# Attention: probabilities turned by VectorE, value products on 32x64 tiles, rope by swap and GpSimd

## The reference

```python
x: (4, 1024, 256), 16 heads, nope 128, rope 64, values 128, rank 64
q = x @ Wqa @ Wqb ; ckv = x @ Wkva
compressed, k_pe = ckv[..., :64], ckv[..., 64:]
kv = compressed @ Wkvb            # k_nope, v for each head
q_pe, k_pe = _rope(q_pe), _rope(k_pe)
scores = einsum('bhnd,bhmd->bhnm', qf, kf) / sqrt(192)
attn = softmax(where(causal, scores, min))
out = einsum('bhnm,bhmd->bhnd', attn, v) ; x = x + out @ Wout
x = x + ffn(layernorm(x))         # 8 groups x 8 experts, top 8
```

## Time and profile before

| | us |
|---|---|
| median of 3 runs | 1732.25 (1731.49 to 1733.08) |
| the profiled execution | 1732.48 |
| its span, first to last instruction | 1730.7 |
| preparation and start, to the first body | 90 |
| first body | 27.2 |
| thirty bodies, 117.2 to 1183.6 us | 1066.4 |
| last scores and router, to 1240 us | 56.4 |
| experts, to the end | 491 |

### The profile page before, as it was taken

The page is one execution under the profiler, slowest core; times in us unless marked ns, Lnnn a source line. Parts: engine busy times, 40 slices in busy tenths (PEclk is TensorE's granted clock), DMA queues, the critical chain, the costliest instruction groups (busy, mean ns, idle before and its releaser), DMA issues.

```text
span 1730.7 us, 31809 instructions
## 1 busy us (share of the span) xinstructions
PE 1662.5 (96%) x11024; PEld 1357.5 (78%) x11024; DVE 1248.5 (72%) x2923; ACT 955.1 (55%) x2255; POOL 509.9 (29%) x433
## 2 busy tenths in 40 slices
PE   5799999999999999999999999999999999999998
PEld 4667777777777777777777777777699999999998
DVE  6888888888888788888888888888654554555543
ACT  6566666666666666666666666666433333433332
POOL 4543334323333333423343333335310110110100
PEclk9899999999999999999999999999999999999999
DMA  8300010012000003000002210001300000000000
GB/s 287 117 26 20 20 32 25 20 47 96 20 25 20 20 32 111 26 20 26 25 26 65 65 32 24 22 19 38 110 1 25 26 1 25 26 14 12 13 13 13
DMA packets 50204, 68.49 MB, mean 40 GB/s; under 512 B 8512, under 2 KB 33088, under 8 KB 50048
## 3 DMA queue, kind: packets, MB, share of 16 engines
q1 hardware_dynamic: 50048, 66.45, 11.6%
HBM read 52.00 MB, written 14.42 MB: 38 GB/s over the span
## 4 chain that ended last, share of the span: by engine, by line
PE 81%; issue 8%; DVE 4%; ACT 2%; DMA 1%; POOL 1%; ACTq 0%; DVEq 0%
PE aps L43 46%; PE fps L43 23%; PE aps L1233 9%; PE fps L1618 2%; ACT probs L1307 1%; DVE f_stats L739 1%; DMA raw_down<-in_down 1%; DVE nmax L1357 0%; POOL rot L1454 0%; PE fps L700 0%; PE fps L668 0%; DVE aTl L1759 0%; DVE rot L1371 0%; DVE aps L1357 0%; DVE rot L792 0%
## 5 line engine op out<-in xcount | busy, mean ns | idle before, releaser
L1307 ACT ACTIVATE probs<-aps,nmax 128x384 f32<-128x384 f32 (+7 forms) x512 | 378.6, 743 | 229.7 <-DVE nmax L1357 224.0
L1357 DVE CUSTOM_DVE_ANT_0 aps<-aps,mask_row 128x384 f32<-128x384 f32 (+7 forms) x512 | 387.2, 772 | 105.9 <-PE aps L43 100.3
L1233 PE MATMUL aps<-ident,probs 128*128 128x128 f32 x2304 | 324.0, 272 | 0.9 <-ACT probs L1307 0.6
L43 PE MATMUL aps<-kTh,qh 128*128 128x512 f32 (+3 forms) x768 | 293.3, 382 | 23.3 <-ACT probs L1307 18.4
L1233 PEld LDWEIGHTS aps<-ident,probs 128*128 128x128 f32 x2304 | 271.7, 140 | 27.2 <-issue 1.5
L1318 ACT COPY pT<-aps 128x512 f32<-128x512 f32 (+3 forms) x485 | 229.5, 504 | 92.1 <-PE aps L1233 89.5
L43 PE MATMUL aps<-pT,v 128*64 128x512 f32 (+3 forms) x1536 | 268.9, 492 | 0.6 <-ACT pT L1318 0.6
L43 PE MATMUL aps<-kTl,qh 128*128 128x512 f32 (+3 forms) x768 | 257.9, 343 | 0.0
L1454 POOL TENSOR_TENSOR rot<-rot 64x512 f32<-64x512 f32 x128 | 163.9, 1280 | 211.8 <-DVE rot L1371 211.8
L43 PE MATMUL aps<-kTh,ql 128*128 128x512 f32 (+3 forms) x768 | 221.8, 343 | 0.0
L43 PEld LDWEIGHTS aps<-pT,v 128*64 128x64 f32 x1536 | 101.7, 136 | 152.1 <-issue 142.1
(11 more groups left out here) (190 smaller groups left out, 2878.1 us busy)
## 6 DMA issues: line engine op xcount, KB each, us to landing
linv_b<-inverses_scratch SPq DMA_DIRECT2D x128, 128.0 KB, 2.8
wqs<-wq_scratch SPq DMA_DIRECT2D x30, 256.0 KB, 3.1
raw_numbers<-in_x SPq DMA_DIRECT2D x8, 512.0 KB, 6.2
acc<-in_x SPq DMA_DIRECT2D x8, 512.0 KB, 4.0
inverses_scratch<-linv_t SPq DMA_DIRECT2D x256, 1.0 KB
x_scratch<-acc SPq DMA_DIRECT2D x8, 512.0 KB, 2.9
x<-x_scratch SPq DMA_DIRECT2D x8, 512.0 KB, 3.9
out<-x SPq DMA_DIRECT2D x7, 512.0 KB, 2.9
```

Of the source, the lines that this page charges most:

```text
L43: return nc.tensor.matmul(out, lhsT, rhs, start=start, stop=stop, skip_group_check=True)
L1233: last = nc.tensor.transpose(tps[:, TS.index(x) % 3, j * P:(j + 1) * P], probs[c][:, c * (pair % 2), a, off:off + P], t.ident[:])
L1307: nc.scalar.activation(probs[c][:, c * (r % 2), a, off:off + w], sps[:, at:at + w], ACT.Exp, bias=nmax[:, c, a, j:j + 1], scale=-1.0, accu ...
L1357: nc.vector.tensor_tensor_reduce(out=s, in0=s, in1=mask[:, N - PW[c][j]:N], scale=-1.0, scalar=3.0e38, op0=ALU.add, op1=ALU.min, accum_out ...
```

## The change

- **Turning.** T and OUT are gone. TURN(c, a, j) on VectorE is one instruction for each score tile: it transposes `probs` in blocks of 32 x 32 from SBUF to SBUF, into `pT_first` or `pT_second`. A 32-row strip of `pT` then holds, for 32 of each 128 tokens, the keys in blocks of 32. `probs` becomes a ring of five tiles.
- **Value products.** The values are held four times, one copy for each 32-row strip (`vrep`), loaded from DRAM in pieces of 256 bytes. A product has 32 rows (keys) and 64 columns (values), and 32 to 128 moving columns; strip a writes bank 4 + a, head h the upper or lower 64 partitions: eight tiles of the array. There are 360 such products in a body (two PE instructions each) where there were 24, and they stand in PV(1, 0 to 7) and PV(0, 0 to 3), twelve pieces of four key blocks. O reads the four banks.
- **Rope.** RAW on ScalarE copies the projection to `rot1`; SWAP, two transfers of 64 KB on SP, crosses the halves into `rot2`; ROT is three instructions of 64 partitions on GpSimd (on VectorE for the first two queries).
- **Transfers.** Keys, values and `acc` move in 256 KB pieces, one or two a body, at set places of SP's list. `acc` is double. All four batches' values go to DRAM.
- **The first expert weights** are split by ScalarE and VectorE in the last body instead of GpSimd.
- All tables are written anew. Scores keep to banks 0 to 3 but for the last tile and the first body.

The core of the diff:

```diff
+    nc.vector.transpose(pT[c][:, a, 0:w // S32, j * S32:(j + 1) * S32],
+                        probs[:, SLOT[EXP(c, a, j), r], 0:w].rearrange("p (b k) -> p b k", k=S32))\
+        .then_inc(p_turned, 1)
...
-                    for kb in range(first, first + n):
-                        for a in range(2):
-                            k = TS.index(T(c, kb, a))
-                            s = t_cols(TS[k])
-                            last = mm(nc, ops[64 * a:64 * a + 64, s:QC], t.v32[:, pair // PAIRS % 2, kb, :],
-                                      pT[:, k % PT_BUFS, s:QC], kb == 0, kb == KB[c] - 1)
+                    if part == 0:
+                        if pair % PAIRS == 0:
+                            pe.wait_ge(values_loaded[b % 2], 64 * (b // 2 + 1))
+                        pe.wait_ge(p_turned, last_of("tr", c, pair))
+                        banks_free(x)
+                    n = BLOCKS[c] // PARTS[c]
+                    for b in range(part * n, (part + 1) * n):
+                        for a in range(4):
+                            s = max(0, b // 4 - 4 * c) * S32
+                            if b // 4 >= 4 * c and b % 4 > a:
+                                s += S32
+                            if s == 4 * S32:
+                                continue
+                            for h in range(2):
+                                last = mm(nc, banks[64 * h:64 * h + 64, OB + a, s:4 * S32],
+                                          vrep[32 * a:32 * a + 32, pair // PAIRS % 2, b, :],
+                                          pT[c][32 * a:32 * a + 32, h, b, s:], b == 0, b == BLOCKS[c] - 1)
...
-                    nc.vector.tensor_tensor(rot1[:, k, :], sps[:, at:at + QC], t.cosT[:, cols], ALU.mult)
-                    for to, source in ((0, 32), (32, 0)):
-                        last = nc.vector.tensor_tensor(rot2[to:to + 32, k, :], sps[source:source + 32, at:at + QC],
-                                                       t.sinT[to:to + 32, cols], ALU.mult)
+                    nc.scalar.copy(rot1[:, rot_slot(x, r), :], banks[:, bank_of(Q(c, a), r), :]).then_inc(q_raw, 1)
...
+            def swap(x, r):
+                sp.wait_ge(q_raw, count(of("raw", x), r))
+                sp.dma_start(rot2[0:32, k, :], rot1[32:64, k, :]).then_inc(q_swapped[k], 16)
+                sp.dma_start(rot2[32:64, k, :], rot1[0:32, k, :]).then_inc(q_swapped[k], 16)
...
+            eng.wait_ge(q_swapped[k], 32 * ((count(of("raw", x), r) + 1) // 2))
+            eng.tensor_tensor(rot2[:, k, :], rot2[:, k, :], t.sinT[:, cols], ALU.mult).then_inc(q_turned, 1)
+            eng.tensor_tensor(rot1[0:64, k, :], rot1[0:64, k, :], t.cosT[0:64, cols], ALU.mult).then_inc(q_turned, 1)
+            eng.wait_ge(q_turned, 2 * n)
+            eng.tensor_tensor(rot1[0:64, k, :], rot1[0:64, k, :], rot2[:, k, :], ALU.add).then_inc(q_add, 1)
...
+            def load_values(b, a):
+                sp.dma_start(vrep[32 * a:32 * a + 32, b % 2], t.v_dram[b].rearrange("(n k) d -> k n d", k=S32))\
+                    .then_inc(values_loaded[b % 2], 16)
...
+        POOL = [ROT(1, 1), ROT(1, 0), LOW(1, 1), LOW(1, 0), ROT(0, 0), ROT(0, 1), OLOW(1), LOW(0, 1), LOW(0, 0),
+                OLOW(0)]
+        SYNC = [SWAP(1, 1), SWAP(1, 0), KEEP(1), SPREAD(1), SWAP(0, 0), KEEP(0), SPREAD(0), SWAP(0, 1)]
```

More of the change, by code:

```diff
@@ L1014, in exists, with body @@
             return 0 <= r + age(x) < B * PAIRS
-        BODIES = range(-1, B * PAIRS + 1)
-        def body(order, first, r):
+        BODIES = range(-1, LAST + 1)
+        def body(order, first, last, r):
+            if r == LAST:
+                return last
             return [x for x in (first if r == 0 else order) if exists(x, r)]
         def tensor_body(r):
-            return body(TENSOR, TENSOR_FIRST, r)
-        TS = [x for x in TENSOR if x[0] == "t"]
-        PVS = [x for x in TENSOR if x[0] == "p"]
@@ new lines, in sync_body @@
+        def sync_body(r):
+            return body(SYNC, SYNC_FIRST, SYNC_LAST, r)
+        SS = [x for x in TENSOR if x[0] == "s"]
+        COUNT, KINDS = {}, {}
+        for bodies in (tensor_body, vector_body, scalar_body, pool_body, sync_body):
+            for r in BODIES:
+                for x in bodies(r):
+                    if x[0] not in ("router", "mask", "stats", "quad"):
+                        KINDS[x[0]] = KINDS.get(x[0], 0) + 1
+                        COUNT[x, r] = KINDS[x[0]]
@@ new lines, in count, with of, at_pair, last_of @@
+        def count(x, r):
+            return COUNT[x, r]
+        def of(kind, x):
+            return (kind,) + x[1:]
+        def at_pair(x, pair):
+            return count(x, pair - age(x))
+        def last_of(kind, c, pair):
+            return max(at_pair(x, pair) for x in TENSOR + VECTOR + SCALAR if x[0] == kind and x[1] == c)
+        RING_USERS = [(x, r) for r in BODIES for x in scalar_body(r) if x[0] == "exp"]
+        SLOT = {y: n % RING for n, y in enumerate(RING_USERS)}
+        def slot_before(x, r):
+            n = RING_USERS.index((x, r))
+            return RING_USERS[n - RING] if n >= RING else None
@@ L1069, in bank_users, with takes_banks @@
+        def takes_banks(x):
+            return x[0] in ("s", "q", "y", "router", "mask") or x[0] == "p" and x[2] == 0
+        USERS = {bank: [(x, r) for r in BODIES for x in tensor_body(r) if takes_banks(x) and bank in banks_of(x, r)]
+                 for bank in range(8)}
         def bank_users(x, r):
@@ new lines, in load_acc, with store_acc, all_added @@
+            def load_acc(b, n):
+                tiles = slice(2 * n, 2 * n + 2)
+                sp.dma_start(acc[:, 1 - b % 2, tiles, :], x_v[b][:, tiles, :]).then_inc(acc_loaded[b % 2], 16)
+            def store_acc(b, n):
+                tiles = slice(2 * n, 2 * n + 2)
+                sp.dma_start(x2_v[b][:, tiles, :], acc[:, 1 - b % 2, tiles, :]).then_inc(x2_stored, 16)
+            def all_added(pair):
+                for c in range(NC2):
+                    sp.wait_ge(y_added, last_of("acc", c, pair))
@@ L1129, in _ @@
+            job = {"spw": keep_inverses, "spr": spread_inverses, "sw": swap}
+            sp.dma_start(mask[:, N - P:N], ins["mask"]).then_inc(mask_loaded, 16)
+            for r in BODIES:
+                if r == 0:
+                    sp.wait_ge(t.values_stored, 32)
+                    for a in range(4):
+                        load_values(0, a)
+                if 1 <= r and r + 1 < LAST:
+                    queries_of_second_half(r - 1)
                     if r <= 2:
@@ L1176, in _ @@
+            scores_of(LAST - 1)
+            queries_of_second_half(LAST - 1)
+            load_experts(nc, t, ins, 1, slice(0, 4))
+            all_added(LAST - 1)
+            for n in range(4):
+                store_acc(B - 1, n)
         @block.tensor
@@ L1477, in run @@
                         router_norm(nc, t, 1, i)
-                for x in body(POOL, POOL_FIRST, r):
+                job = {"rot": rot_job, "low": low_job, "olow": olow_job, "stats": stats_job}
+                for x in pool_body(r):
                     job[x[0]](x)
-                    if r == LAST - 1 and x == LOW(1, 0):
-                        pool.wait_ge(q_ps, max(count(Q(1, a), LAST - PAIRS - 1) for a in range(2)))
+                    if r == LAST - 1 and x == [y for y in pool_body(r) if y[0:2] == ("low", 1)][-1]:
+                        pool.wait_ge(q_ps, max(at_pair(Q(1, a), LAST - PAIRS - 1) for a in range(2)))
                         router_root(nc, t, 0)
```

599 lines of the change are left out of this document (288 added, 311 removed).

## The result

The changed kernel takes 1660.5 us (median of 4 runs, 1657.6 to 1665.4) against 1732.3 us: ratio 0.959 (0.957 to 0.961). The forecast was 1588 us. So it is faster, inside the range and on the side that was given 0.78, but only half as much as forecast: 72 us instead of 144. The profiled execution took 1660.9 us. One of the four executions of the variant fetch_b (2047.8 us, granted clock 0.65) was in a slower state of the chip and is left out.

The account below looks back on a forecast made before the run. TensorE sets the body period, 35.5 us falling to 30.9 (30.35 + 0.2 + 0.35); over 31 bodies 143 us, last body -4, start +3: 1732.5 - 144 = 1588 us. Range 1540 to 1750, the forecast's own bounds 1540 to 1640.

Parts of the forecast that it names:

- rival A: TensorE in each piece: tiles do not overlap enough; with four at once the kernel takes about 1787 us; chance 0.08.
- rival B: VectorE's turns cost two cycles a column, 37.4 us a body and the bound, kernel 1790 us; chance 0.06.
- D: Full queues: VectorE at 92% in strict order, waits for it leave bodies of 33 to 35 us, 1655 to 1715; chance 0.08.
- The low end for the tiles: TensorE's 720 value-product instructions cost 7.7 us a body, all eight tiles at once, against 28.2 with only two.
- together 11.5 us: New value products on TensorE per body: 7.7 us columns, 0.4 for 32-column blocks, 3.4 for nine visits.
- nine visits: TensorE's separate entries into the narrow shape in a body: 0.38 us each, 3.4 us.
- the diagonal blocks: Eight 32-column blocks on TensorE, whose 27 ns may be shorter than the load of 64 weights: 0.4 us.
- the prediction's own signs of being wrong: PE waiting on turns or low parts in every body, or narrow visits costing more than 0.4 us each.
- rows 5: Cited TensorE trace rows: four tiles at once, four products lasting 0.43 us together, weight loads some 7 ns a pair.
- 0.8 + 0.2 + 0.35: Idle in the forecast period, us: PE's old idle 0.8, query chain 0.2, costlier hand-overs with VectorE at 92% 0.35.
- rival C: Rope chain before the second-half scores becomes the path, 12.6 us against 12.7 of cover: 1620 to 1680 us; chance 0.20.
- 4.6 us to 31 bodies: Period falling from 35.5 to 30.9 us, counted for 31 bodies: 143 us in sum.

Follow-up runs that it names:

- fetch_b: Changed kernel, implied TensorE waits dropped, body padded to 6.5 blocks of 256 instructions, 100 more instructions ahead of the first scores: 1646.0 us (ratio 0.951).
- narrow: Changed kernel with all value products but those of block 0 cut to their last 32 columns: 1666.8 us, one execution.
- slow_low: even_c with the low part of the second half's first query computed twice on GpSimd: 1682.1 us (ratio 0.971).
- joined: Changed kernel with the pieces of value products in six visits instead of nine: 1708.8 us (ratio 0.987).
- even_c: Changed kernel with fulfilled waits padding a body to exactly 7 blocks (1792 instructions), 68 more instructions ahead of the first scores: 1644.8 us (ratio 0.949).
- fetch_a: Changed kernel, implied TensorE waits dropped, body padded to 6.5 blocks of 256 instructions, 56 more instructions ahead of the first scores: 1643.7 us (ratio 0.950).

## Why the prediction was half right

**Bound and mechanism, right.** TensorE sets the period before and after. All eight tiles run at once (rival A out: 0.89 us for a joined piece, not 1.7). A turn costs about one column per step and not two (rival B out):

```profile
L1453 DVE STREAM_TRANSPOSE pT_second<-probs 128x1024 f32<-128x1024 f32 x60 | 74.4, 1240 | 0.0
L1453 DVE STREAM_TRANSPOSE pT_first<-probs 128x256 f32<-128x256 f32 x60 | 25.3, 422 | 0.2 <-issue 0.2
```

That is (1240 - 422)/768 = 1.07 ns a column (forecast 1.05). GpSimd's low parts last 1.285 us beside the turns, as its instructions of this kind did before (1.28), and the 82 that overlap a turn as long as the 44 that don't (1.285 and 1.286), so the turns do not hold it up. The Trainium skill ("SBUF — State Buffer", section "Who interferes with whom") says that a VectorE instruction with at most one SBUF input, outside its two-port modes, does not contend with GpSimd; the trace agrees. VectorE is loaded 26.8/32.65 = 82%, not 92, and TensorE waits for softmax 0.2 us a body, so D is out. The low end for the tiles was right, too: the narrow products start 13.9 ns apart over a joined piece (0.89 us for 64), 7.8 in narrow. The Trainium skill ("TensorE: Matmul & The Clock Gate", section "Wait — 56ns, not 53.3ns?") says that starts never come closer than about 25 ns; these rows disagree, for products on different tiles.

**The step that failed: the cost of the value products on TensorE**, "together 11.5 us". In a body without a stop they cost 13.33 us: columns 7.7 as forecast, nine visits at 0.48 instead of 0.38 (+0.9), and the diagonal blocks 1.3 instead of 0.4 (+0.9). A visit over 0.4 us was one of the prediction's own signs of being wrong, and it came. The visit's price was read from two shapes that had other neighbours; this shape's first sixteen loads and products cost more. The 0.4 was priced at a single weight load, while rows 5 held a figure for the feed ("some 7 ns a pair in a burst") that I held only against the full 128-column pieces. At 8 to 10 ns an instruction the half-empty pieces would have come out about right. That makes 1.8 us a body; a body missed by 1.75.

**The term that was not there: TensorE's own instructions.** 720 narrow instructions with their loads double and more than double TensorE's program (1675 instructions a body; the whole kernel before fetched 93 blocks, this one 240). The stops cost 21.9 us in thirty bodies, 0.7 us each, and the prediction had no term for them. In the sum they are offset by what I had kept as idle, 0.8 + 0.2 + 0.35 = 1.35 us: TensorE is idle 1.08 us now, two thirds of it these stops, and the old hand-over waits have nearly gone. So 30.9 + 1.8 - 0.27 = 32.4; 0.2 us of 32.65 I can't assign.

**The query chain (rival C)**: "cover without slack; I book 0.2" was right. Less than 0.1 was paid, and slow_low shows that from there on all is paid. It was right by luck in one respect: four visits lie in the cover, and with visits as cheap as forecast the cover would have been 0.4 us shorter and the chain late by as much. The chances for C and for the forecast were not independent.

**First and last bodies.** I credited 4.6 us to 31 bodies; only 29 got theirs. The first two and the last pair cost 1.2 us more, where 9 less were forecast. In the last body -4 was forecast and +7.7 came. From the last score to the first product of the experts, before, then after:

```profile
1203.30:1213.70 10.40, 10.39 (x84) 8.51 (x83) 6.51 (x19) 6.82 (x13) 6.01 (x7) 1.00 0.12 33
1213.70:1224.30 10.60, 9.80 (x65) 5.30 (x63) 5.41 (x24) 4.79 (x12) 6.31 (x5) 1.00 0.34 123
1224.30:1231.50 7.20, 5.21 (x54) 3.38 (x53) 4.90 (x10) 2.87 (x6) 1.28 (x1) 1.00 0.28 91
```

```profile
1125.00:1130.07 5.07, 3.78 (x29) 3.10 (x27) 5.07 (x10) 3.41 (x7) 1.28 (x1) 1.00 0.35 129
1130.07:1136.80 6.73, 5.83 (x96) 5.36 (x96) 4.40 (x15) 2.98 (x5) 2.67 (x4) 0.80 0.24 62
1136.80:1148.50 11.70, 6.88 (x425) 6.43 (x424) 8.41 (x27) 0.42 (x1) 3.57 (x3) 0.94 0.30 116
1148.50:1160.90 12.40, 8.26 (x57) 4.86 (x55) 4.93 (x11) 3.20 (x7) 1.26 (x1) 0.76 0.14 44
...
PE aps L46 <- issue: 4.8, 2, 2.8
PE fps L46 <- PEq L848: 3.7, 1, 3.7
```

Seven pieces in one row (1136.8 to 1148.5) hold two stops, 4.8 us together. The granted clock is 0.80 in the stage ahead of them and 0.76 in the one behind, where it was 1.00 before: it is at its lower level, 1.2 GHz, from 1134.1 to 1137.5 us, after four waits for VectorE of 2.2 us together, and from 1147.7 to 1154.5, right after the two stops. What of the 7.7 us is the clock's and what the waits' is not separated. The clock is lower in the first body, too: 0.91 in place of 1.00.

Sum of the misses: 29 pairs x 1.74 = 50, the pairs at the ends 10, the start 0.5, the last body 12, less 1 at the experts: 72 us.

## What to carry to other kernels

When a change multiplies an engine's instructions, price three things beside the columns: the smallest time of one instruction, the entry into and exit from the new shape for each place in the order where it stands, and the supply of instructions. The last shows in a trace as "issue" inside a row of like instructions; count the engine's program in blocks, check the count against the packets of the instruction queue, and see whether the stops end at one place. And a gain per body belongs only to bodies that have the full pattern on both sides: price the first and the last by themselves, the granted clock with them.

## What the runs showed of the chip that I had not expected

TensorE's instructions arrive in packets of 256 (16 KB, about 1 us each, 1.6 us at most). In the bodies of the changed kernel a packet starts when TensorE has 95 to 250 instructions left to the place where the stops end (median 168), and TensorE never passed that place less than 2.15 us after the packet's start. Where these instructions pass faster, as in pieces, TensorE stands, always at the same place of a block. With equal work, the place alone moved the kernel by 33.6 us of 1645.

Second, the kernels with the most stops (joined and narrow) had the most stretches at the lower clock, but which wait lowers it is not shown. Between its third pair and its last, joined (53 us of stops, 34 of softmax waits) had six stretches of 3.4 to 6.8 us at the lower level and even_c (1.6 and 3.8 us) none. The changed kernel had one, at 437.7 us, as TensorE came out of a softmax wait of 2.0 us, and none at its stops of up to 1.5 us in these bodies; in its first body one begins at 116.9 us, 0.5 us behind a stop of 1.8 us.

Third, a fulfilled wait is not free. Instructions of two such waits follow each other 0.106 us apart on TensorE. The 100 of fetch_b take 10.6 us ahead of its first scores, where the query takes 7.8 us anyway, and the first body comes 3 us later than in fetch_a; the 56 of fetch_a and the 69 of even_c fit in and cost nothing there (first score at 80.7 and 80.1 us).
